# Expert tiles ordered by image pair; 28 of 32 images turned and stored in quarters between the tiles

## The reference, cut to what matters

```python
x = x + conv(_ln_c(x), ...)             # stage A, per image
t = _to_tokens(x)                        # 32768 tokens of 128
xf = _ln_t(t)
top_w, top_i = top_k(xf @ Wg + bg, 2)    # two of 8 experts, softmax of the two
for e in range(8):
    h = gelu(xf @ W1[e] + b1[e])         # 128 -> 512
    out += w_dense[:, e:e+1] * (h @ W2[e] + b2[e])
x = _from_tokens(t + out, x)             # back to images, channel first
```

## Time and profile before

| | us |
|---|---|
| median of 3 runs | 1591.4 |
| the profiled execution | 1590.5 |
| its span | 1588.5 |
| tile loop on PE, first `up` to last `down` | 611.1 to 1496.1 |
| output stage, first load to the end | 1503.5 to 1588.5 |

### The profile page before, as it was taken

One profiled execution on the slowest core, in us unless ns is written; L12 is line 12 of the kernel. 1 busy time (PEld: TensorE's weight loads), 2 busy tenths in 40 slices (PEclk: granted clock), 3 DMA queues, 4 the chain that ended last, 5 costly groups with the idle time before them and its releaser, 6 DMA issues.

```text
span 1588.5 us, 45185 instructions
## 1 busy us (share of the span) xinstructions
PE 1468.3 (92%) x12192; PEld 1128.6 (71%) x12193; DVE 1372.5 (86%) x2715; ACT 1064.8 (67%) x2402; POOL 963.8 (61%) x1057
## 2 busy tenths in 40 slices
PE   5899999999998768999999999999999999999765
PEld 2445455444545416999999999999999999999654
DVE  2568888888888866999999999999999999999654
ACT  4577777777777415777777777777777777777400
POOL 1004555446545675777777777777777777777500
PEclk7999999999999757999999999999999999999866
DMA  4202121212221172111111111111111111110199
GB/s 136 80 27 68 59 78 65 71 57 78 64 71 47 40 146 72 44 43 45 47 47 45 43 40 46 43 47 41 47 47 43 48 42 47 47 45 12 40 408 398
DMA packets 61998, 115.70 MB, mean 73 GB/s; under 512 B 15471, under 2 KB 39051, under 8 KB 61946
## 3 DMA queue, kind: packets, MB, share of 16 engines
q1 hardware_dynamic: 37210, 62.14, 12.8%
q0 software_dynamic: 18112, 34.27, 6.8%
q10 hardware_dynamic: 6624, 18.69, 3.2%
HBM read 60.08 MB, written 58.48 MB: 75 GB/s over the span
## 4 chain that ended last, share of the span: by engine, by line
POOL 33%; issue 27%; PE 23%; ACT 8%; DMA 5%; DVE 2%; POOLq 1%; SPq 1%; ACTq 0%; DVEq 0%
POOL token_out L505 17%; PE psV L820 12%; POOL yt L500 7%; POOL xn L493 7%; PE psV L771 4%; DMA ye<-token_out 4%; ACT spent L601 3%; PE psT L805 2%; PE psA L762 2%; PE psG L807 2%; POOL rows_by_pair L475 2%; ACT cv L589 1%; PE psV L999 1%; ACT sq L557 1%; DMA stage<-in_L_ffn_W_dram 1%
## 5 line engine op out<-in xcount | busy, mean ns | idle before, releaser
L1311 DVE TENSOR_TENSOR gl<-g,gh 128x512 f16<-128x512 f32 x620 | 519.9, 878 | 16.5 <-ACT gh L705 8.9
L505 POOL DMA_INDIRECT token_out<-yt,rt x310 | 391.1, 1262 | 185.0 <-POOL yt L500 132.7
L475 POOL DMA_INDIRECT rows_by_pair<-rows,idx x256 | 268.8, 1050 | 325.8 <-issue 202.4
L820 PE MATMUL psV<-lp,diag 128*128 128x512 f32 x576 | 275.3, 610 | 19.0 <-ACT cv L589 17.6
L705 ACT ACTIVATE gh<-g 128x512 f16<-128x512 f32 x465 | 274.5, 624 | 16.9
L698 ACT ACTIVATE g<-psT 128x512 f32<-128x512 f32 x310 | 181.9, 597 | 107.0 <-DVE gl L1311 77.9
L698 ACT ACTIVATE g<-psV 128x512 f32<-128x512 f32 x310 | 184.0, 597 | 90.5 <-PE psV L939 78.9
L960 PE MATMUL psR<-wall,gh 128*128 x1240 | 221.3, 273 | 0.6 <-DVE ya L1328 0.6
L960 PE MATMUL psG<-wall,gh 128*128 x1240 | 221.3, 273 | 0.0
L961 PE MATMUL psG<-wall,gl 128*128 x1240 | 213.0, 219 | 0.0
L961 PE MATMUL psR<-wall,gl 128*128 x1240 | 213.0, 219 | 0.0
(11 more groups left out here) (210 smaller groups left out, 2938.9 us busy)
## 6 DMA issues: line engine op xcount, KB each, us to landing
rt<-rows_by_pair SPq DMA_DIRECT2D x155, 133.0 KB
xb<-in_x_dram SPq DMA_DIRECT2D x32, 512.0 KB, 3.5
ye<-token_out SPq DMA_DIRECT2D x32, 512.0 KB, 7.9
out_dram<-oe ACTq DMA_DIRECT2D x32, 512.0 KB, 8.5
token_out<-yt,rt POOLq DMA_INDIRECT x310
rows_by_pair<-rows,idx POOLq DMA_INDIRECT x256, 2.4
stage<-in_L_ffn_W_dram SPq DMA_DIRECT2D x1, 2048.0 KB, 9.6
rows_by_pair<-pad_rows SPq DMA_DIRECT2D x15, 133.0 KB
```

The costliest lines, as they stand in the source:

```text
L475: gp.indirect_dma_start(rows_dram, bass.IndirectOffsetOnAxis(ap=idx[p][:, b:b + 1].bitcast(U32), axis=0), rows[p][:, b, :], None).then_inc ...
L505: gp.indirect_dma_start(y_dram, bass.IndirectOffsetOnAxis(ap=rt[r][:, b, ID:ID + 1].bitcast(U32), axis=0), yt[r][:, b, :], None, bounds_ch ...
L820: ins = te.matmul(psConv.rearrange("p (h w) -> p h w", w=WW), diag[k][:, m, :], lp[j][:, y:y + HH // 2, dx:dx + WW], start=(m == 0), stop= ...
L1311: v.tensor_tensor(gl[side][q][:, cols], g[side][:, cols], gh[side][q][:, cols], ALU.subtract).then_inc(lo_done, 1)
```

## The change

The queue holds the same tiles of the same lists, but ordered by the pair of images that a tile's first row belongs to, and by list within one pair of images. For that the running counts are kept per pair of images (`hist`, a new 28 columns each time), and the table is worked out from 16 x 32 cells in place of 28. The table no longer goes through DRAM: PE multiplies its three columns with the identity into psA, and DVE copies the row from there.

Images 0 to 27 are turned in quarters (256 pixels, 128 KB): SP loads quarter m in its turn m+48, PE transposes it in step m+44 (`turn_quarter`), ACT copies it out of psA in the same step (`out_quarter`), and SP stores it in its turn m+54. Steps 44 to 154 and one after the loop hold the 112 quarters. The last four images go through the old way, with psV and psT in place of psA and psV.

```diff
+    Q_SP, Q_PE = 48, 44
...
             def turnover(j, r, t):
+                    first = sp.value_load(tab[0:1, j:j + 1] ...)
+                sp.wait_ge(y_out[r], 16 * TB * t)
+                    load_rows(first, r)
+                    sp.wait_ge(oq_done, j - lag + 3)      # lag = Q_SP + 6
+                    store_quarter(c, n)
+                        sp.wait_ge(xT_ready, j - Q_SP + Q_PE)
+                    load_quarter(c, n)
...
+                if j - RING == NT - 1 - NB2 // TB:
+                    load_image(NIMG - 4)
+                    load_image(NIMG - 3)
+            load_image(NIMG - 2)
+            load_image(NIMG - 1)
...
+            def out_quarter(j, r):
+                act.wait_ge(xT_ready, j + 4)
+                act.wait_ge(oq_out[c], 4 * j - 4 * c - 4 * Q_PE + 16)
+                sc_.activation(oq[c][:, :], psA[:, ...:... + QTR], ACT.Copy).then_inc(oq_done, 1)
...
+            def turn_quarter(j, r):
+                c, at = r % 4, 512 * ((r + 3) % 2) + T
+                pe.wait_ge(yq_in[c], 4 * j - 4 * c - 4 * Q_PE + 16)
+                for b in range(2):
+                    last = te.transpose(psA[:, at + b * P:at + (b + 1) * P], yq[c][:, b, :], ident[:, :])
...
+            for n, col in enumerate((trow, ta, tb_)):
+                for c in range(NT_COLS):
+                    last = te.matmul(psA[0:1, ...], col[:, c:c + 1], ident[:, :], start=True, stop=True)
...
+            dve.wait_ge(tab_turned, 1)
+            v.tensor_scalar(tab[:, :], psA[0:1, 0:n], float(T), None, ALU.mult)
+            for side in range(2):
+                last = v.tensor_scalar(tab_off[...], psA[0:1, ...], float(EW), None, ALU.mult)
```

More of the change, by code:

```diff
@@ L89, in conv_moe_block @@
     NT_COLS = -(-NT // P)
+    KS = 32
+    QF = (NIMG // 2) * KS
+    QTR = 2 * P
+    NQ = 4 * (NIMG - 4)
+    Q_SP, Q_PE = 48, 44
+    assert 4 * NBLK == KS and KS >= NPAIR and PIX == 4 * QTR
     RW = D + 5
@@ L343, in _ @@
         def _(sp):
-            for free in o_out:
+            for free in oq_out:
                 sp.sem_inc(free, 16)
+            sp.sem_inc(oq_done, 2)
             def load(n, q):
@@ L421, in _ @@
-            for j in range(4):
[L422 to L428, removed]
+            for j in range(Q_SP, Q_SP + RING):
+                turnover(j, j % RING, j // RING)
+            with sp.Fori(Q_SP // RING + 1, ROUNDS, 1) as t:
+                for r in range(RING):
+                    turnover(RING * t + r, r, t)
@@ L710, in dstep @@
                     gelu(j + 1, 0, r + 1)
+                if images:
+                    out_quarter(j, r)
                 if not last or j + 3 < NT:
@@ L720, in _ @@
             for j in range(BODY):
-                dstep(j, j)
-            with act.Fori(1, NT // BODY - 1, 1) as t:
+                dstep(j, j, False)
+            with act.Fori(1, Q_PE // BODY, 1) as t:
                 for r in range(BODY):
-                    dstep(BODY * t + r, r)
+                    dstep(BODY * t + r, r, False)
+            with act.Fori(Q_PE // BODY, NT // BODY - 1, 1) as t:
+                for r in range(BODY):
+                    dstep(BODY * t + r, r, True)
             for j in range(BODY * (NT // BODY - 1), NT):
[L726 to L732, removed]
+                dstep(j, j, True)
+            for j in range(NT, Q_PE + NQ):
+                out_quarter(j, j)
+            for j in range(4):
+                act.wait_ge(o_ready, j + 1)
+                act.dma_start(out_v[NIMG - 4 + j], oe[j][:, :]).then_inc(o_out[j], 16)
         @block.tensor
@@ L924, in turn_rows @@
                     last = te.transpose(psA[:, 512 * (r % 2) + b * P:512 * (r % 2) + (b + 1) * P], xn[r % 4][:, b, :], ident[:, :])
-                last.then_inc(xT_ready, 1)
+                return last
+            def turn_quarter(j, r):
+                c, at = r % 4, 512 * ((r + 3) % 2) + T
+                pe.wait_ge(yq_in[c], 4 * j - 4 * c - 4 * Q_PE + 16)
+                if isinstance(j, int) and j + 3 >= NT:
+                    pe.wait_ge(oq_done, j - Q_PE + 1)
+                    pe.wait_ge(xl_done, min(j + 2, NT))
+                for b in range(2):
+                    last = te.transpose(psA[:, at + b * P:at + (b + 1) * P], yq[c][:, b, :], ident[:, :])
+                return last
             def up(j, side, r):
@@ L965, in down, with dstep @@
                 last.then_inc(y_ready, 1)
-            def dstep(j, r):
+            def dstep(j, r, images):
                 last = isinstance(j, int)
@@ L971, in dstep @@
                 if not last or j + 3 < NT:
-                    turn_rows(j + 3, r + 3)
+                    turned = turn_rows(j + 3, r + 3)
+                if images:
+                    turned = turn_quarter(j, r)
+                if images or not last or j + 3 < NT:
+                    turned.then_inc(xT_ready, 1)
                 down(j, 0, r)
@@ L981, in _ @@
             for j in range(3):
-                turn_rows(j, j)
+                turn_rows(j, j).then_inc(xT_ready, 1)
             up(0, 0, 0)
@@ L985, in _ @@
             for j in range(BODY):
-                dstep(j, j)
-            with pe.Fori(1, NT // BODY - 1, 1) as t:
+                dstep(j, j, False)
+            with pe.Fori(1, Q_PE // BODY, 1) as t:
                 for r in range(BODY):
-                    dstep(BODY * t + r, r)
+                    dstep(BODY * t + r, r, False)
+            with pe.Fori(Q_PE // BODY, NT // BODY - 1, 1) as t:
+                for r in range(BODY):
+                    dstep(BODY * t + r, r, True)
             for j in range(BODY * (NT // BODY - 1), NT):
[L991 to L1000, removed]
+                dstep(j, j, True)
+            for j in range(NT, Q_PE + NQ):
+                turn_quarter(j, j).then_inc(xT_ready, 1)
+            pe.wait_ge(g_done, 4 * NT)
+            for j in range(4):
+                pe.wait_ge(ye_in[j], 16)
+                if j >= 2:
+                    pe.wait_ge(o_ready, j - 1)
+                for b in range(NBLK):
+                    last = te.transpose(hbank[j % 2][:, b * P:(b + 1) * P], ye[j][:, b, :], ident[:, :])
+                last.then_inc(yT_ready, 1)
         @block.vector
@@ L1167, in place @@
                 dve.wait_ge(pairs_ready, st_.count(4, 1, 1))
-                link(v.tensor_tensor(pos[:, :, :], psR[:, 0:R_CNT].rearrange("p (b k) -> p b k", k=NPAIR), per_blk(base, NPAIR), ALU.add))
-                v.tensor_tensor(base[:, :], base[:, :], psR[:, R_CNT:R_CNT + NPAIR], ALU.add).then_inc(rank_read, 1)
+                at = st_.count(4, NPAIR, 0)
+                now, after = ((hist[:, a:a + NPAIR] if st_.fixed else hist[:, bass.ds(a, NPAIR)]) for a in (at, at + NPAIR))
+                link(v.tensor_tensor(pos[:, :, :], psR[:, 0:R_CNT].rearrange("p (b k) -> p b k", k=NPAIR), now.unsqueeze(1).broadcast_to([P, NB2, NPAIR]), ALU.add))
+                v.tensor_tensor(after, now, psR[:, R_CNT:R_CNT + NPAIR], ALU.add).then_inc(rank_read, 1)
             def number(st_):
@@ L1248, in _ @@
             dve.wait_ge(idx_ready, NU)
[L1249 to L1254, removed]
@@ new lines, in _ @@
+            link(v.scalar_tensor_tensor(out=seen, in0=seen, scalar=-1.0, in1=seen, op0=ALU.mult, op1=ALU.max))
+            link(v.tensor_scalar(seen, seen, float(T - 1), None, ALU.add))
+            link(v.tensor_copy(spare, seen))
+            link(v.tensor_scalar(spare, spare, T.bit_length() - 1, None, ALU.arith_shift_right))
+            link(v.tensor_copy(up_to[:, KS:KS + QF].rearrange("p (s k) -> p s k", k=KS)[:, :, 0:NPAIR], spare.rearrange("p (s k) -> p s k", k=NPAIR)))
+            link(v.tensor_tensor(new, up_to[:, KS:KS + QF], up_to[:, 0:QF], ALU.subtract))
@@ L1272, in _ @@
+            link(v.scalar_tensor_tensor(out=trow[:, :], in0=down_[:, :], scalar=float((CAP - T - NUP * CAP) // T), in1=trow[:, :], op0=ALU.mult, op1=ALU.add))
+            link(v.tensor_tensor(trow[:, :], trow[:, :], over[:, :], ALU.max))
+            link(v.tensor_scalar(trow[:, :], trow[:, :], float(NREG * CAP // T), None, ALU.min))
             link(v.memset(ta[:, :], 0.0))
```

136 lines of the change are left out of this document (76 added, 60 removed).

## The result

| | before | after |
|---|---|---|
| median of 4 runs | 1591.51 us | 1544.49 us |
| lowest to highest | 1590.75 to 1591.75 | 1542.34 to 1545.35 |
| profiled execution | 1590.5, span 1588.5 | 1543.75, span 1541.5 |

The ratio is 0.9703, with a 95% interval from 0.9688 to 0.9717: 47 us less, where 1544.5 us was forecast. That a forecast hits the median to 0.01 us is luck: its terms were off by 0.3 to 1.1 us, in both directions, and the runs of one kernel lie up to 3 us apart.

The account below looks back on a forecast made before the run. The prediction took PE to bound the tile loop and transfers the output stage. 1590.5 - 73.3 (output) + 24.4 (quarters) + 1.5 (table) + 0.5 (counts) = 1543.6, plus 0.9 to the median: 1544.5 us, range 1540 to 1567.

Parts of the forecast that it names:

- What bounds: Tile loop bound by PE, without a gap in its 5.71 us step; output stage bound by transfers.
- The output stage: Behind the last scatter: 85.04 us removed, 11.7 us left for the last two images, gain 73.3.
- Rival 3: End of kernel: the last two images' load and store take 7.85 us each, 1553.8 us; chance 0.08.
- The quarters on PE: Loop steps 44 to 154: two added transposes cost 0.22 us a step, 24.4 us in all.
- The copy on ACT: Loop: the quarter's 0.37 us copy out of PSUM fits ACT's 0.69 us gap and adds nothing.
- DVE as a second bound: Loop: DVE, busy 693 of 700 us, has almost no slack in a step of 5.71 us.
- rival 2: Loop: ACT's copy isn't hidden and DVE sets the step, 5.71 + 0.42 us, giving 1566.7; chance 0.10.
- rival 5: Loop: a quarter isn't there when PE wants it, needing a landing above 23.7 us; with the rest, chance 0.01.
- SP: Loop: three issues at 1.07 us take 3.2 us of a 5.93 us step, covered, adding nothing.
- The table: Before the loop: table products and copies move the loop's start by 0.2 to 3 us, 1.5 taken.
- The counts per image pair: Stage A's loop: two register instructions per pair of images, 0 to 2.7 us, 0.5 taken.
- The sum: Whole kernel: 1590.5 - 73.3 + 24.4 + 1.5 + 0.5 = 1543.6, with 0.9 to the median 1544.5 us; chance 0.73.

## Why the prediction was right, point by point

**What bounds.** Right. PE has no gap in the loop before and after, and the kernels with one and four transposes show that the time follows PE's step alone.

**The output stage.** 73.3 was forecast, 73.6 came. Each of the five pieces (load 3.3, transposes 2.0 and 1.8, copy 1.2, store 3.3) was within 0.1 us of its row. Rival 3, the crowded load of 7.85 us, is out: only two images move, and the load took 3.26. Images 28 and 29 are turned at 1522.83 to 1524.7, while POOL still scatters, as said.

**The quarters on PE.** 24.4 forecast, 24.1 measured, and 0.11 per transpose held from one to four. Here the prediction had chosen between two prices, the row's 0.11 and the duration of 0.273. The Trainium skill gives the duration ("TensorE: Matmul & The Clock Gate", Part 4, PE-mode transpose: about 275 ns in a kernel's context). It agrees with the row, and it isn't what a transpose costs a step in which others stand next to it. Nor did the granted clock fall: it is 1.00, the higher of the two levels (2.4 GHz), in the loop's window with 4 transposes among the 64 instructions of a step.

**The copy on ACT.** Hidden, as forecast, and not narrowly. The timeline of ACT in the changed kernel, answering to the earlier trace rows:

```profile
1001.27 0.36 ACT L722 ACTIVATE oq<-psA 128x256 f32<-128x256 f32 x1
1001.53 0.38 ACT L715 ACTIVATE xh<-psA 128x256 f16<-128x256 f32 x1
1002.54 1.17 ACT L732 ACTIVATE g<-psT 128x512 f32<-128x512 f32 x2 [0.64 <-DVE gl L1390]
```

The copy stands ahead of the high half, and ACT still waits 0.64 us for DVE before its next gelu. It had waited 0.69.

**DVE as a second bound.** This premise of rival 2 was wrong. The prediction read DVE's 693 of 700 us as "almost no slack". The groups by line from 900 to 1400 us, first of the kernel before (columns as in the earlier trace rows; `gl` is the gelu's low half, on POOL stands the scatter):

```profile
L1311 DVE TENSOR_TENSOR gl<-g,gh 128x512 f16<-128x512 f32 x352 | 300.1, 892 | 5.0 <-ACT gh L705 1.2
L505 POOL DMA_INDIRECT token_out<-yt,rt x176 | 227.7, 1294 | 105.2 <-POOL yt L500 75.8 <-issue 29.4
```

and of the changed one:

```profile
L1390 DVE TENSOR_TENSOR gl<-g,gh 128x512 f16<-128x512 f32 x338 | 268.3, 832 | 42.1 <-ACT gh L739 37.9 <-issue 1.3
L532 POOL DMA_INDIRECT token_out<-yt,rt x169 | 185.9, 1100 | 101.4 <-POOL yt L527 73.2 <-issue 28.2
...
L981 PE MATMUL psA<-ident,yq 128*128 128x128 f32 x168 | 32.1, 272 | 0.0
```

In a step that is 4% longer the same instruction became 7% shorter, and DVE's idle time ahead of it rose from 5.0 to 42.1 us. Its 99% was partly stretched work. The last row is the quarter's transposes, without idle time: rival 5 is out too.

**SP.** Hidden, as forecast. The price of 1.07 per issue, from twelve row loads in 12.82 us, was twice too high, since each of those loads came with a read of the table; an issue alone is 0.52, and the turn 2.3 in place of 3.2. It was an error on the safe side, in a term that counted as nothing.

**The table.** The chain on DVE ends at 588.84 (589 forecast) and is hidden behind the shift products, which run until 601.5. The products take 2.7 us (1.5 to 3.0 forecast), and the low halves run from 605.24 to 610.1 (609 to 611). The term that was mis-sized is the step from there to the loop: 1.5 was taken, and the first `up` came at 613.14 in place of 611.05, 2.1 later. Before, PE waited for POOL's rows and not for the low halves, as the prediction read it; now the low halves are so late that the loop's start goes by their end, with POOL's first tile ready just behind it (the rows on the table as transposes show it). On top come 0.5 us that the prediction didn't have. In the kernel before, PE's products are at the higher clock level (granted clock 1.00, 2.4 GHz) from the row

```profile
613.17 0.27 PE L938 MATMUL psV<-xl,wall 128*128 128x256 f16 x1
```

on, 2.1 us after the first `up`; in the changed kernel from 616.34 on, 3.2 us after it. Until then the granted clock is 0.50, the lower level (1.2 GHz), and they start 0.21 us apart and not 0.11. That is 15 products at the wide spacing in place of 10, at 0.10 each 0.5. What made the rise come later isn't settled. The two kernels with the table as transposes moved it further, to 22 and 23 products, without being made for that.

**The counts per image pair.** Forecast 0.5, and nothing of it can be seen: the table's first instruction on DVE starts at 569.99 against 570.03. These are single executions; in the traces of the other kernels, whose stage A is the same as the changed one's, it starts between 569.1 and 571.1, so 0.5 can't be told from nothing.

**The sum.** By the span: forecast -73.3 + 24.4 + 1.5 + 0.5 = -46.9; measured -73.6 + 24.1 + 2.1 + 0.5 (clock) + 0 = -46.9, against -47.0 in the profiled executions. What was missing at the loop's start (2.6 in place of 1.5) was offset by the counts, the quarters and the tail.

## What to carry to other kernels

Where two stages have different limits, the work of the one costs the other only what it adds to that one's bound: 73.6 us of transfers and turning became 24.1 us of PE, and the rest vanished behind it. Price an added instruction by the distance between the starts of neighbours of its kind in the timeline, on PE and on ACT alike, and not by its duration. And before a high busy share is called a second bound, look whether the durations on that engine are stretched by another one.

## What the runs showed of the hardware that was not expected

- DVE's op on two inputs in SBUF fell from 892 to 832 ns and POOL's scatter from 1294 to 1100 ns when the step grew from 5.71 to 5.92 us, while POOL's normalising of a tile (`xn`) rose from 604 to 752. With a single transpose per quarter (5.81 us) `gl` is already at 821 and the scatter at 1096 from 1000 to 1400 us; with the order alone (5.70 us) they are at 891 and 1300. DVE's and POOL's work in a step is the same in both, so the amount of work on these two engines doesn't explain it; that it is which instructions fall together is likely, but not shown. The Trainium skill says that POOL's way to SBUF is shared with DVE and contended when DVE reads two inputs from SBUF ("GPSIMD Engine Reference", 1. Specifications); the rows agree with that, but no run took one of the two away, so the cause is not shown. The nearest to it is POOL's first instruction of the loop, 2.06 us beside DVE's low halves (two inputs in SBUF each) and 0.44 each for those that follow. In all eleven traces with the new table it ends 0.3 us behind the last low half.
- An issue on SP's queue takes 0.52 us, so that nine of them fit into a step of 5.92 us.
- The granted clock at the loop's start rose from 0.50 to 1.00 2.1 us after the first product in the kernel before, 2.9 to 3.6 in the nine traces with the table as products, and 4.65 and 4.89 in the two with the table as transposes. Ahead of it PE's instructions were the same in the kernel before, the changed one and the one with transposes: three pairs of transposes, and before them over 6.7 us without work. The cause stays open.
